# Attention loop of a two-layer vision tower: VectorE's steps of pairs p and p-2 interleaved, TensorE's values ahead of its transposes, ScalarE's masked values ahead of its exponent

## What is computed

```python
scores = einsum('bhqd,bhkd->bhqk', q, k) * SCALE      # 16 heads of 16, 37 tokens an image
attn   = softmax(scores, axis=-1)                      # layer 0: masked above the diagonal
out    = einsum('bhqk,bhkd->bqhd', attn, v)
```

## Time and profile before

| | us |
|---|---|
| median of 3 runs | 400.12 (399.53 to 401.8) |
| profiled execution | 399.5 |
| its span, first to last instruction | 397.5 |
| PE, DVE, ACT, POOL busy | 353.9, 202.0, 129.6, 78.3 |

### The profile page before, as it was taken

The page is one execution under the profiler, slowest core; times in us unless marked ns, Lnnn a source line. Parts: engine busy times, 40 slices in busy tenths (PEclk is TensorE's granted clock), DMA queues, the critical chain, the costliest instruction groups (busy, mean ns, idle before and its releaser), DMA issues.

```text
span 397.5 us, 8324 instructions
## 1 busy us (share of the span) xinstructions
PE 353.9 (89%) x3185; PEld 298.9 (75%) x3185; DVE 202.0 (51%) x584; ACT 129.6 (33%) x301; POOL 78.3 (20%) x118
## 2 busy tenths in 40 slices
PE   7699599799789999999488999877699999999994
PEld 5586386577678999998356677645499999999993
DVE  5658844986745032112865587776732242232334
ACT  2414173675012534422035477122111111112220
POOL 1212118730113201004213440011140000000041
PEclk9699599999956999999979999957699999999999
DMA  7999811000792493262790000590034888708823
GB/s 270 258 350 415 345 60 64 2 0 2 246 406 71 144 357 99 78 222 84 265 397 2 2 0 0 209 418 10 2 112 142 307 311 317 315 28 342 320 61 96
DMA packets 20742, 70.85 MB, mean 178 GB/s; under 512 B 4386, under 2 KB 13172, under 8 KB 15716
## 3 DMA queue, kind: packets, MB, share of 16 engines
q1 hardware_dynamic: 19028, 65.81, 44.6%
q0 software_dynamic: 1680, 4.59, 3.3%
HBM read 61.62 MB, written 7.56 MB: 174 GB/s over the span
## 4 chain that ended last, share of the span: by engine, by line
PE 60%; DVE 24%; ACT 4%; DMA 4%; issue 3%; POOL 3%; SPq 1%; DVEq 0%; POOLq 0%; ACTq 0%
PE psum L1142 21%; PE psum L1151 14%; PE psum L586 4%; PE psum L1121 3%; DVE srec L773 3%; PE psum L545 2%; DVE sc L767 2%; DVE smax L763 2%; PE psum L580 2%; PE psum L911 2%; DMA wp_s<-Wp 2%; PE psum L697 2%; POOL rstd L1485 1%; PE psum L478 1%; PE psum L497 1%
## 5 line engine op out<-in xcount | busy, mean ns | idle before, releaser
L1142 PEld LDWEIGHTS psum<-xwT,arena 128*128 128x128 f32 x736 | 84.3, 192 | 1.1 <-issue 0.5
L1142 PE MATMUL psum<-xwT,arena 128*128 128x128 f32 x736 | 84.7, 275 | 0.1
L1151 PE MATMUL psum<-arena,prob 128*128 128x256 f32 x272 | 61.5, 379 | 0.0
L1151 PEld LDWEIGHTS psum<-arena,prob 128*128 128x128 f32 x272 | 50.4, 190 | 6.1
L545 PE MATMUL psum<-causal_b,identb 128*128 128x296 bf16 x286 | 50.4, 327 | 2.5 <-DVE arena L632 0.9
L1285 ACT ACTIVATE act_a<-psum 128x128 f32<-128x128 f32 x72 | 20.0, 278 | 84.9 <-PE psum L1142 84.3
L1211 DVE TENSOR_TENSOR prob<-psum,act_a 128x128 f32<-128x128 f32 x72 | 21.0, 292 | 43.9 <-ACT act_a L1285 43.9
L545 PEld LDWEIGHTS psum<-causal_b,identb 128*128 128x128 bf16 x286 | 29.3, 110 | 16.3 <-DMA xd_z<-slots_out,slot_gi 1.3
L1278 ACT ACTIVATE prob<-psum,par_s 128x128 f32<-128x128 f32 x64 | 23.6, 368 | 38.8 <-PE psum L1142 34.4
L1036 POOL DMA_DIRECT2D slots_out<-zw x15 | 8.3, 552 | 128.8 <-DVE zw L1222 83.2
L773 DVE RECIPROCAL srec<-psum 128x148 f32<-128x148 f32 x16 | 17.3, 1080 | 9.5 <-PE psum L713 9.4
(11 more groups left out here) (217 smaller groups left out, 530.0 us busy)
## 6 DMA issues: line engine op xcount, KB each, us to landing
arena<-w SPq DMA_DIRECT2D x28, 1024.0 KB, 10.4
arena<-w SPq DMA_DIRECT2D x10, 2048.0 KB, 8.4
arena<-xp SPq DMA_DIRECT2D x5, 384.0 KB, 6.6
xw<-slots_in SPq DMA_DIRECT2D x15, 128.0 KB, 4.2
slots_out<-zw POOLq DMA_DIRECT2D x15, 128.0 KB, 6.8
slots_in<-zero SPq DMA_DIRECT2D x1, 1792.0 KB, 11.3
slots_out<-zero SPq DMA_DIRECT2D x1, 1792.0 KB, 15.2
arena<-arena SPq DMA_DIRECT2D x16, 74.0 KB, 1.9
```

The lines of the kernel that those rows point to most:

```text
L1142: last = nc.tensor.matmul(bank(1 + f % 4)[:, part * WIN:(part + 1) * WIN], w1v[:, k, part * FF + f * P:part * FF + (f + 1) * P], rows[:, k ...
L1151: last = nc.tensor.matmul(bank(into)[:, 0:D], hid[:, f, :], w2v[:, f, :], start=(f == 0), stop=(f == FC - 1))
```

## The change

On VectorE `softmax_vector` and `output_vector` are each cut in two, and the loop runs maximum(p), reciprocal of the sums (p-2), shift(p), product(p-2). On TensorE the loop runs scores(p), outputs(p-2), transposes(p-1). On ScalarE the masked values of p-1 come first in `step(p)`, ahead of the exponent of p and its waits. No instruction is added or removed, and every wait keeps its semaphore and count.

```diff
                         scores_tensor(pe, p, b)
+                        output_tensor(pe, p - 2, b)
                         turn_probs_tensor(pe, p - 1, 1 - b)
-                        output_tensor(pe, p - 2, b)
...
-                        softmax_vector(dve, p, b)
+                        maximum_vector(dve, p, b)
+                        sums_vector(dve, p - 2, b)
+                        shift_vector(dve, p, b)
                         output_vector(dve, p - 2, b)
-                output_vector(dve, PAIRS - 2, 0)
-                output_vector(dve, PAIRS - 1, 1)
+                for b in range(2):
+                    sums_vector(dve, PAIRS - 2 + b, b)
+                    output_vector(dve, PAIRS - 2 + b, b)
...
                 def step(p, buf):
+                    if not (isinstance(p, int) and p == 0):
+                        mask_values_scalar(act, p - 1, 1 - buf)
                     act.wait_ge(s("sc_read"), done + p + 1)
...
-                    if not (isinstance(p, int) and p == 0):
-                        mask_values_scalar(act, p - 1, 1 - buf)
                     act.wait_ge(s("pT_ps"), done + p + 1)
```

More of the change, by code:

```diff
@@ L757, in tensor, with maximum_vector @@
                 finish(4)
-            def softmax_vector(dve, p, buf):
+            def maximum_vector(dve, p, buf):
                 heads = lambda a: a.rearrange("p r (n k) -> p r n k", k=SEQ)
@@ L763, in softmax_vector, with shift_vector @@
                 nc.vector.reduce_max(smax[:, buf], heads(scores_psum(buf)), AX.X).then_inc(s("smax"), 1)
+            def shift_vector(dve, p, buf):
+                heads = lambda a: a.rearrange("p r (n k) -> p r n k", k=SEQ)
                 dve.wait_ge(s("smax"), done + p + 1)
@@ L769, in softmax_vector, with sums_vector, output_vector @@
                                         ALU.subtract).then_inc(s("sc_read"), 1)
-            def output_vector(dve, p, buf):
+            def sums_vector(dve, p, buf):
                 dve.wait_ge(s("o_ps"), done + p + 1)
                 nc.vector.reciprocal(srec[:], bank(6 + buf)[:, DC * PW:2 * DC * PW]).then_inc(s("srec"), 1)
+            def output_vector(dve, p, buf):
                 dve.wait_ge(s("srec"), done + p + 1)
@@ L790, in vector @@
                 for p in range(2):
-                    softmax_vector(dve, p, p)
+                    maximum_vector(dve, p, p)
+                    shift_vector(dve, p, p)
                     nc.vector.memset(srec[:, 0:1], 0.0).then_inc(s("o_read"), 1)
```

## The result

The changed kernel takes 407.87 us (median of 4 runs, 406.4 to 410.51) against 400.96 us for the kernel before in the same session. The ratio is 1.018 with a 95% interval of 1.011 to 1.025: slower by 4 to 10 us. A median here is that of all runs of a kernel, while a ratio compares fast runs alone, so the two need not agree to the last digit. The forecast was 409.0 in a range of 405.0 to 413.0. The profiled execution took 407.81 us, 8.3 more than the profiled one of before.

A forecast was written before the change was run, and what follows sets the result against it. TensorE and VectorE were taken as nearly full; a new TensorE-ScalarE chain of 4.18 us a pair would bound the loops. Layers' +3.6 and +5.2 give +8.8 on 399.5, 408.3; as a median 409.0, range 405.0 to 413.0.

The forecast's parts named there:

- The ring: Attention loops: transposes, copy to pT, masked values, outputs, next transposes take 4.18 us a pair, against 3.41 and 3.49; chance 0.82.
- Transposes to copy: Attention loops: from the start of TensorE's transposes to the start of ScalarE's copy to pT, 1.11 us a turn.
- copy to next: ScalarE in the attention loops: from the copy to pT to the next instruction, the masked values, 0.92 us a turn.
- the outputs: TensorE in the attention loops: from the start of the outputs to the next instruction, the transposes, 1.21 us a turn.
- the hand-over from ScalarE to TensorE: Attention loops: from the end of the masked values to the start of the outputs, 0.05 us a turn.
- Start, turns, end: Attention up to pair 7's transposes: layer 0 +0.9, +3.1, -0.4 (together +3.6); layer 1 +2.0, +2.8, +0.4 (together +5.2).
- VectorE's order in the loop: Attention loops: VectorE itself saves 0.1 to 0.2 us a pair, but this falls on no path.
- The exponent and the shift under cover: Attention loops: exponent hidden in the outputs' 1.21 us; shift done after 3.2 us, ScalarE reaching the exponent after 4.0.
- The branch on ScalarE: Loop branch between copy and masked values: hidden behind the 1.02 us copy, 0; if exposed, +1.2 us in all.
- The clock behind attention: Routing behind attention: clock change taken as 0, with 2 us either side; 3.7 us could be given back or lost.
- TensorE did not stay the bound: Rival, attention loops: masked values off the path, TensorE still the bound, 399.5 to 400 us or some 396; chance 0.06.
- The clock did not fall: Rival, attention loops: idle TensorE loses its clock, 1.9 us a turn more, 418 and up to 427 us; chance 0.06.

The follow-up runs named there:

- e1: Changed kernel, but ScalarE makes each pair's masked values ahead of that pair's own copy to pT; 394.48 us, ratio to before 0.990.
- e2: Changed kernel with VectorE's old order, shift of p ahead of the reciprocal of p-2; 404.66 us, ratio to before 1.017.
- e9: Kernel before with 30 instead of 16 warm-up matmuls between layer 0's attention and its routing; 397.85 us, ratio to before 0.995.
- e3: Changed kernel with ScalarE's old order, masked values of p-1 behind the exponent of p; 414.82 us, ratio to before 1.041.
- e5: Changed kernel with two more copies of the masked values' size a pair on ScalarE ahead of them; 420.64 us (one run).
- e8: Kernel of e1 with the copy to pT in two halves and one warm-up matmul a pair; 393.81 us, ratio to before 0.991.
- e4: Changed kernel with TensorE's old order, transposes of p-1 ahead of outputs of p-2; two runs, 409.59 and 418.50 us.

## Why the prediction was right, step by step

- **The ring.** Costed 4.18 us, measured 4.24. Transposes to copy 1.11 and copy to next 0.92 were exact, masked values 0.89 too; the outputs took 1.17 (238.67 to 239.84) instead of 1.21. The step that was mis-sized is the hand-over from ScalarE to TensorE: 0.15 (238.52 to 238.67), where I took 0.05 from an exponent ahead of transposes. In run e1 the same outputs started 0.05 behind the copy; why they start later behind the masked values no run shows.
- **Start, turns, end.** Layer 0: +0.55, +3.31, -0.48 (forecast +0.9, +3.1, -0.4). Layer 1: +2.14, +2.99, +0.34 (forecast +2.0, +2.8, +0.4). Sum 8.85, forecast 8.8. That the sum is closer than its pieces is luck: the turns cost 0.4 more than forecast, and the start of layer 0 0.35 less. There VectorE's reciprocal started 0.68 us behind the maximum and the shift 0.99 behind the reciprocal, where 0.81 and 1.05 were taken, and the shift took 0.70 instead of 0.78.
- **What was costed at nothing.** VectorE's order in the loop: nothing, by run e2 (0.07 us of attention). The exponent and the shift under cover: yes, by the timelines above. The branch on ScalarE: nothing, since turns with and without it are alike (4.24, 4.25, 4.23).
- **The clock behind attention.** Taken as unchanged: in the profiled runs it was, 12.80 us against 12.85. The medians moved by 6.9 us, less than the attention's 8.85; the profiled runs show 1.2 us of the difference behind layer 1's attention. Run e9's time is some 2 us under before's, and the stage between the attentions took 128.2 to 128.3 us in the three traces with the lower clock there and 124.8 to 126.1 in the others: that is the size for which the range was widened.
- **The rivals.** TensorE did not stay the bound: it waits 0.83 to 0.97 us a turn. The clock did not fall in the changed kernel's loop, but it did in runs e1, e3, e5 and e8, in each behind longer waits (1.50 to 2.46 us). The rule of the Trainium skill that was weighed (TensorE: Matmul & The Clock Gate, A second HAM failure mode: psum-queue depth-cycling) agrees with the traces of e3 and e5, where the clock swings between 0.50 and 1.00 within the loop, and not with those of the changed kernel and of e4. The prediction's price of 1.9 us a turn was an upper end: e3's slow turns are 0.6 to 0.9 us longer, because of the slower matmuls only the transposes (1.92 instead of 1.07) lie on the ring; the warm-ups and scores go into the wait behind them, which falls from about 1.5 to between 0.5 and 1.0. The prediction did not say how long a wait would bring a fall about, and the runs do not settle it either: there are falls behind 1.50 us and none behind 1.87 and 2.15.

## What to carry to other kernels

When a wait is moved between two engines that each run in program order, write down the ring of instructions through both queues that returns to its start one iteration later, and add it up: it bounds the loop however idle both engines are. An instruction that is on no path today (the masked values) gets onto it as soon as its consumer is moved ahead, so ask of each input of a moved step where its producer stands in its queue. Compare variants by the stage that the change touches as well as by the total, since a clock that changes elsewhere can hide or add several microseconds.

## What the runs showed of the hardware beyond that

- TensorE kept a granted clock of 1.00 through two loops in which it was 77 and 80% busy with waits of 0.83 to 0.97 us a turn; in e4, 72 and 71% busy with waits of 1.40 to 1.43 us a turn, it kept 1.00 too; in e3 and e5, behind waits of 1.50 to 1.77 us, it fell to about 0.50 again and again. Single waits of 1.87 us (before) and 2.15 us (changed) brought no fall, one of 1.90 us (e1) did, so the length of a wait is not all that counts; what else does, no run shows.
- With 14 more small matmuls in an idle stretch of 2 us the routing's matmuls behind them took 8.61 us in the trace, against 12.85 before, and the time fell by some 2 us (ratio 0.995). Other traces had the higher clock there without them.
- Two ScalarE copies of 74x512 out of psum took 1.07 us from the first start to the last end, one of 74x1024 took 1.02: cutting the copy cost 0.05 us, and the first half started 0.67 us behind the start of its transposes instead of 1.11.
